# Biases of two small attention stages on VectorE, the shared expert summed in parts, routing weights carried with the expert rows

## The reference, cut to what matters

```python
# first attention: queries, and a second, small attention over the last 16 context rows
kv_dca = (y_dca @ Wkv_dca + bkv_dca).reshape(b, DCA, 2, H, HD)
k_dca = _ln(kv_dca[:, :, 0], kn_dca_w, kn_dca_b)
v_dca = kv_dca[:, :, 1]
q = _ln((x @ Wq + bq).reshape(b, s1, H, HD), qn_w, qn_b)
...
ctx = ctx + DCA_WEIGHT * _attn(qT, k_dca, v_dca)
# experts: top 2 of 16 for each token, at most 128 rows for each expert, and a shared expert
out = jnp.einsum('eci,edi->ecd', h, W2).astype(xt.dtype)
y_pairs = out[e, posc] * (w.reshape(-1) * valid)[:, None]
y = y_pairs.reshape(T, K, D).sum(axis=1)
shared = (silu(xt @ Ws1.T) * (xt @ Ws3.T)) @ Ws2.T
return y + shared
```

## Time and profile before

| | |
|---|---|
| time, median of 3 runs | 2241.15 us (2239.74 to 2242.74) |
| the profiled execution's own time | 2241.21 us |
| its span, first to last instruction | 2239.4 us |
| PE busy | 2004.3 us, 90% of the span |
| DVE busy | 1730.4 us, 77% |
| ACT busy | 1229.3 us, 55% |
| POOL busy | 1258.4 us, 56% |
| the three stages touched, first queries, small attention, experts | 37.6, 67.4 and 121 us long |

### The profile page before, as it was taken

How to read it: one execution, slowest core, us unless ns; L and a number is a source line. 1 busy time by engine, 2 the same in 40 slices (tenths; PEclk the granted TensorE clock), 3 DMA queues, 4 the chain that set the end, 5 groups by cost and what they waited for, 6 DMA issues and landing times. The chain is left out here.

```text
span 2239.4 us, 48991 instructions
## 1 busy us (share of the span) xinstructions
PE 2004.3 (90%) x17910; PEld 1649.8 (74%) x17910; DVE 1730.4 (77%) x2549; ACT 1229.3 (55%) x2124; POOL 1258.4 (56%) x1031
## 2 busy tenths in 40 slices
PE   6999999999999767999988785878999999999775
PEld 3788788878887555777777543657999999999763
DVE  5788888788888666888886434859899999999577
ACT  2788888888888513565655212664444444444443
POOL 0666666666666404545452041544898989898450
PEclk9999999999999866999999777989999999999988
DMA  2524222332332322434341343584222323231230
GB/s 87 175 99 167 113 113 112 153 128 98 130 135 115 129 73 90 176 126 168 133 153 58 116 135 90 158 209 143 102 102 103 109 94 116 81 118 38 90 128 17
DMA packets 117615, 262.18 MB, mean 117 GB/s; under 512 B 48033, under 2 KB 87106, under 8 KB 108338
## 3 DMA queue, kind: packets, MB, share of 16 engines
q1 hardware_dynamic: 113634, 248.88, 31.7%
q10 hardware_dynamic: 2304, 7.34, 0.8%
q0 software_dynamic: 1536, 3.94, 0.5%
HBM read 154.89 MB, written 109.20 MB: 118 GB/s over the span
## 5 line engine op out<-in xcount | busy, mean ns | idle before, releaser
L384 DVE TENSOR_REDUCE rk<-n_sq 128x1024 f32 (+2 forms) x384 | 465.8, 1213 | 124.1 <-ACT n_sq L332 121.6
L332 ACT ACTIVATE n_sq<-n_slot 128x1024 f32<-128x1024 f32 (+1 forms) x384 | 394.4, 1027 | 135.5 <-PE n_slot L292 126.3
L290 PE MATMUL n_slot<-n_wh,n_yh 128*128 128x512 f32 (+1 forms) x768 | 318.6, 415 | 2.0 <-PEq L485 2.0
L292 PE MATMUL n_slot<-n_wh,n_yl 128*128 128x512 f32 (+1 forms) x768 | 303.4, 395 | 0.0
L291 PE MATMUL n_slot<-n_wl,n_yh 128*128 128x512 f32 (+1 forms) x768 | 302.0, 393 | 0.0
L1441 POOL TENSOR_TENSOR p_S<-p_S,a_mb 128x896 f32<-128x896 f32 x94 | 255.3, 2754 | 68.0 <-ACT a_mb L1486 68.0
L1813 DVE TENSOR_REDUCE a_mpart<-a_pre 112x1 f32<-112x512 f32 (+1 forms) x384 | 238.7, 668 | 46.5 <-PE a_pre L1644 43.5
L1441 POOL TENSOR_TENSOR a_S<-a_S,a_mb 128x896 f32<-128x896 f32 (+1 forms) x89 | 240.7, 2741 | 39.5 <-ACT a_mb L1486 39.5
L1747 ACT ACTIVATE a_pr<-a_sc 128x896 f32<-128x896 f32 x192 | 171.8, 917 | 150.7 <-PE a_sc L1673 150.7
L264 POOL TENSOR_TENSOR n_khat<-n_kb,n_rs 128x240 f32<-128x240 f32 x192 | 114.7, 597 | 234.7 <-DVE n_rs L399 234.6
L1499 ACT ACTIVATE p_S<-p_S 128x896 f32<-128x896 f32 x96 | 91.5, 953 | 161.3 <-POOL p_S L1441 158.0
(11 more groups left out here) (395 smaller groups left out, 4729.9 us busy)
## 6 DMA issues: line engine op xcount, KB each, us to landing
vdram<-n_v SPq DMA_DIRECT2D x16, 1632.0 KB, 5.3
a_v<-vdram SPq DMA_DIRECT2D x16, 1632.0 KB, 6.7
kTdram<-n_kT SPq DMA_DIRECT2D x16, 1484.0 KB, 5.0
a_kT<-kTdram SPq DMA_DIRECT2D x16, 1484.0 KB, 7.5
n_yT<-in_ctxT SPq DMA_DIRECT2D x16, 750.0 KB, 9.1
yhdram<-n_yh SPq DMA_DIRECT2D x16, 750.0 KB, 6.4
yldram<-n_yl SPq DMA_DIRECT2D x16, 750.0 KB, 8.5
a_yh<-yhdram SPq DMA_DIRECT2D x16, 750.0 KB, 4.2
```

Of the source, the lines that this page charges most:

```text
L290: pe.matmul(dst, high, wh[:, cols], start=True, stop=False)
L292: mm = pe.matmul(dst, low, wh[:, cols], start=False, stop=True)
L332: act.activation(sq[0:n, w, :], slot[w][0:n, :], ACT.Square).then_inc(slot_free, 1)
L384: dve.tensor_reduce(g.rk[0:n, b, j, 8 * s:8 * s + 8], sq[0:n, (2 * j + s) % 3, :].rearrange("p (h d) -> p h d", h=8), X, ALU.add)\
```

## The change

It has five parts.

1. **First queries**: the bias matmul (512) goes; DVE adds the bias while it moves the bank into `z` (new function `bias`), ACT squares `z` instead of the bank, and the order of DVE's and ACT's steps is written anew. PE no longer waits for the table of ones; POOL does, in the next phase.
2. **Small attention, bias**: the bias matmul (670) goes; DVE adds a bias that is now stored on all 128 partitions.
3. **Small attention, loads**: `ydT`, `wkd`, `wvd` and the bias row are loaded by `load_splits` in the first layer norm, in front of the router's tables, and live until the small attention.
4. **Masked keys**: DVE makes half 0; half 1 is made by ACT in eight copies, one for each head, with the head's mask as a scale.
5. **Experts**: part 0 of the shared expert is multiplied for all 8 tiles before part 1, into four banks, and DVE adds two tiles at once; the routing weight travels as one more column of each row, is copied into `slot_w` beside the number, and is applied by ACT as it moves the expert's result; the last sums become four plain additions of four tiles each. POOL's scatter waits for the weights too, and SP's and ACT's waits for `pair_ready` count two copies for each expert.

```diff
-    for dst, src in ((g.blk, "blk"), (g.hmask, "hmask"), (g.bkdrow, "bkd")):
+    for dst, src in ((g.blk, "blk"), (g.hmask, "hmask")):
         sp.dma_start(dst[tuple(slice(None) for _ in dst.shape)], g.a[src]).then_inc(g.consts_in, 16)
+    for dst, src in ((g.ydT, "ydT"), (g.wkd, "L0_Wkd"), (g.wvd, "L0_Wvd"), (g.bkdrow, "bkd")):
+        sp.dma_start(dst[:, :], g.a[src]).then_inc(g.small_in, 16)
...
-                        pe.matmul(dst, g.xnT[:, k, t * TT:(t + 1) * TT], g.wqa[:, k, :], start=(k == 0), stop=False)
-                    mm = pe.matmul(dst, g.ones[0:1, 0:TT], g.qrow[0:1, 0, :], start=False, stop=True)
+                        mm = pe.matmul(dst, g.xnT[:, k, t * TT:(t + 1) * TT], g.wqa[:, k, :], start=(k == 0), stop=(k == 1))
...
+            def bias(s):
+                dve.wait_ge(q_psum, s + 1)
+                dve.tensor_tensor(of(z, s), ps[s][0:TT, :].rearrange("p (a n) -> p a n", a=GT),
+                                  g.qrow[0:TT, 0:1, :].broadcast_to([TT, GT, D]), ALU.add).then_inc(biased, 1)
...
-                pe.matmul(pt[:, t * D:(t + 1) * D], ydT[:, t * P:(t + 1) * P], wkd[:, :], start=True, stop=False)
-                mm = pe.matmul(pt[:, t * D:(t + 1) * D], g.ones[0:1, :], g.bkdrow[0:1, :], start=False, stop=True)
+                mm = pe.matmul(pt[:, t * D:(t + 1) * D], ydT[:, t * P:(t + 1) * P], wkd[:, :], start=True, stop=True)
...
+            act.wait_ge(kT_ready, 2)
+            for h in range(8):
+                act.activation(km[:, 1, :, h, :], kT[:, 1, :].rearrange("p (b k) -> p b k", b=B), ACT.Copy,
+                               scale=g.hmask[:, h:h + 1]).then_inc(km_ready, 1)
...
+            pool.wait_ge(w_ready, 1)
...
+            for t in range(NT):
+                pe.matmul(shared_out(t), hs[0][:, t * TT:(t + 1) * TT], w2a[:, E, :], start=(t % 2 == 0), stop=False,
+                          skip_group_check=True)
             pe.wait_ge(sh_steps, 8)
             for t in range(NT):
-                if t >= 2:
-                    pe.wait_ge(sh_added, t - 1)
...
+                mm = pe.matmul(shared_out(t), hs[1][0:FB, t * TT:(t + 1) * TT], w2b[:, E, :], start=False, stop=True,
+                               skip_group_check=True)
+                if t % 2 == 1:
+                    mm.then_inc(sh_out, 1)
+            pe.wait_ge(sh_added, NT // 2)
...
-                    act.activation(ye[1 - i][:, :], bY[1 - i][:, 0:D], ACT.Copy, scale=0.5).then_inc(y_ready, 1)
+                    act.activation(ye[1 - i][:, :], bY[1 - i][:, 0:D], ACT.Copy,
+                                   scale=slot_w[:, e:e + 1] if isinstance(e, int) else slot_w[:, bass.ds(e, 1)]).then_inc(y_ready, 1)
...
+                    dve.tensor_copy(slot_w[:, n:n + 1] if isinstance(n, int) else slot_w[:, bass.ds(n, 1)],
+                                    xe[i][:, D + 1:D + 2]).then_inc(pair_ready, 1)
...
-                    dve.scalar_tensor_tensor(out=g.x[:, t, :], in0=yg[:, k, t, :], scalar=w[:, k, t:t + 1],
-                                             in1=g.x[:, t, :], op0=ALU.mult, op1=ALU.add).then_inc(summed, 1)
+                    dve.tensor_tensor(g.x[:, tiles, :], g.x[:, tiles, :], yg[:, k, tiles, :], ALU.add).then_inc(summed, 1)
```

More of the change, by code:

```diff
@@ L243, in _ @@
             pool.wait_ge(set_up, 6)
+            pool.wait_ge(g.ones_in, 16)
             def step(b, i, pair):
@@ L556, in _ @@
             square(2)
+            root(2)
             high_part(0)
             square(3)
-            root(2)
             root(3)
@@ L605, in low_part @@
                                          op0=ALU.add, op1=ALU.subtract).then_inc(split, 1)
+            bias(0)
             sums(0)
+            bias(1)
             normalise(0)
             sums(1)
+            bias(2)
             normalise(1)
+            sums(2)
             low_part(0)
-            sums(2)
+            bias(3)
+            normalise(2)
             sums(3)
-            normalise(2)
             low_part(1)
@@ L632, in phase_dca @@
         S = lambda n: g.sem(f"d_{n}")
-        ydT, wkd, wvd = sb("ydT", [P, NKD]), sb("wkd", [P, D]), sb("wvd", [P, D])
+        ydT, wkd, wvd = g.ydT, g.wkd, g.wvd
         yrep = sb("yrep", [P, B, 8, DCA])
@@ L658, in _ @@
         def _(sp):
-            sp.dma_start(ydT[:, :], g.a["ydT"]).then_inc(y_in, 16)
-            sp.dma_start(wkd[:, :], g.a["L0_Wkd"]).then_inc(w_in, 16)
-            sp.dma_start(wvd[:, :], g.a["L0_Wvd"]).then_inc(w_in, 16)
             load_first_keys(sp, g)
@@ L787, in _ @@
                                   ALU.mult, ALU.mult).then_inc(kT_ready, 1)
-            dve.wait_ge(kT_ready, 2)
-            for half in range(2):
-                dve.tensor_tensor(km[:, half, :, :, :],
-                                  kT[:, half, :].rearrange("p (b k) -> p b k", b=B).unsqueeze(2).broadcast_to([P, B, 8, DCA]),
-                                  g.hmask[:, :].unsqueeze(1).unsqueeze(3).broadcast_to([P, B, 8, DCA]), ALU.mult)\
-                   .then_inc(km_ready, 1)
+            dve.wait_ge(kT_ready, 1)
+            dve.tensor_tensor(km[:, 0, :, :, :],
+                              kT[:, 0, :].rearrange("p (b k) -> p b k", b=B).unsqueeze(2).broadcast_to([P, B, 8, DCA]),
+                              g.hmask[:, :].unsqueeze(1).unsqueeze(3).broadcast_to([P, B, 8, DCA]), ALU.mult)\
+               .then_inc(km_ready, 1)
             p3 = lambda n: pr[n % 2][:, :, :, :].rearrange("p b h k -> p (b h) k")
@@ L2042, in phase_moe @@
         w2a, w2b = sb("w2a", [P, E + 1, D]), sb("w2b", [FB, E + 1, D])
-        xe = [sb(f"xe{i}", [P, D + 1]) for i in range(2)]
+        xe = [sb(f"xe{i}", [P, D + 2]) for i in range(2)]
         xeT, ye = [[sb(f"{n}{i}", [P, 2 * P]) for i in range(2)] for n in ("xeT", "ye")]
@@ L2340, in _ @@
             dve.wait_ge(side, 14)
-            dve.tensor_tensor(a3(w), a3(w), den[:, :].unsqueeze(1).broadcast_to([TT, 2, NT]), ALU.mult).then_inc(side, 1)
+            dve.scalar_tensor_tensor(out=rows[:, :, :, D + 1], in0=a3(w), scalar=0.5,
+                                     in1=den[:, :].unsqueeze(1).broadcast_to([TT, 2, NT]), op0=ALU.mult,
+                                     op1=ALU.mult).then_inc(w_ready, 1)
             for part in range(2):
@@ L2353, in _ @@
                     dve.tensor_tensor(h_, h_, ps[3 + half][0:m, 0:HALF], ALU.mult).then_inc(sh_steps, 1)
-            for t in range(NT):
-                dve.wait_ge(sh_out, t + 1)
-                dve.scalar_tensor_tensor(out=g.x[:, t, :], in0=ps[5 + t % 2][0:TT, 0:D], scalar=0.5, in1=g.x[:, t, :],
-                                         op0=ALU.mult, op1=ALU.add).then_inc(sh_added, 1)
+            for m in range(NT // 2):
+                dve.wait_ge(sh_out, m + 1)
+                xs = g.x[:, 2 * m:2 * m + 2, :]
+                dve.scalar_tensor_tensor(out=xs, in0=ps[SHARED[m]][0:TT, :].rearrange("p (a n) -> p a n", a=2), scalar=0.5,
+                                         in1=xs, op0=ALU.mult, op1=ALU.add).then_inc(sh_added, 1)
             def step(n, pair, i):
@@ L2384, in _ @@
                 pass
-            for t in range(NT):
+            for n in range(2):
+                tiles = slice(4 * n, 4 * n + 4)
+                dve.wait_ge(gathered[n], 32)
                 for k in range(2):
-                    dve.wait_ge(gathered[t // 4], 32)
-                    if t or k:
-                        dve.wait_ge(summed, 2 * t + k)
-                    dve.scalar_tensor_tensor(out=g.x[:, t, :], in0=yg[:, k, t, :], scalar=w[:, k, t:t + 1],
-                                             in1=g.x[:, t, :], op0=ALU.mult, op1=ALU.add).then_inc(summed, 1)
+                    if k:
+                        dve.wait_ge(summed, 2 * n + 1)
+                    dve.tensor_tensor(g.x[:, tiles, :], g.x[:, tiles, :], yg[:, k, tiles, :], ALU.add).then_inc(summed, 1)
 def ternary_weights(nc, g, ctx):
@@ L2680, in build @@
             with nc.sbuf_tensor("qs0", [P, T], F32) as qs0, nc.sbuf_tensor("qs1", [P, T], F32) as qs1, \
-                    nc.sbuf_tensor("cols", [P, 8], F32) as g.cols:
+                    nc.sbuf_tensor("cols", [P, 8], F32) as g.cols, nc.sbuf_tensor("ydT", [P, B * DCA], F32) as g.ydT, \
+                    nc.sbuf_tensor("wkd", [P, D], F32) as g.wkd, nc.sbuf_tensor("wvd", [P, D], F32) as g.wvd, \
+                    nc.sbuf_tensor("bkdrow", [P, D], F32) as g.bkdrow:
                 g.qs = [qs0, qs1]
@@ L2739, in laid_out @@
         "low": np.triu(np.ones((TT, TT), np.float32), 1),
[L2740 removed]
+        "L0_Wk": wk0, "L0_Wkd": wkd, "L0_Wvd": wvd, "ydT": i["ctx_1024"][:, SEQ - DCA:].transpose(2, 0, 1).reshape(C, B * DCA), "bk0": np.broadcast_to(bk0, (P, D)), "bkd": np.broadcast_to(bkd, (P, D)),
         "sel": sel, "den1": den1, "cols0": cols,
```

58 lines of the change are left out of this document (29 added, 29 removed).

## The result

The changed kernel takes 2217.99 us (median of 4 runs, 2216.02 to 2219.50), against 2240.44 for the kernel before, measured beside it: a ratio of 0.9899, 95% interval 0.9884 to 0.9914. The forecast was 2217.5. The profiled execution of the changed kernel took 2219.1 us, with a span of 2217.3, so the two traces differ by 22.1 us, and the table accounts for it. Every boundary in it is the first instruction of its kind in the trace.

The account below looks back on a forecast made before the run. Taken as last: PE in the first queries and small attention, PE's shared-expert matmuls in the experts, DVE in the last sums. Terms -5.6, -4.9, -1.3, -7.9, -4.1, +0.1 sum to -23.7 us; from 2241.21 that gave 2217.5, range 2211 to 2224.

Parts of the forecast that it names:

- First queries, gross: First queries without bias matmuls: DVE becomes last, the last reciprocal comes earlier; 7.0 us gained before the longer SP list.
- SP's list: Layer norm: three more load issues by SP put the first queries back by 1.4 us.
- Small attention: Its start: PE begins 3.3 us earlier, two bias matmuls save 2.3, a DVE step adds 0.72; net -4.9 us.
- The masked keys: Small attention: ACT's eight copies take 3.2 us beside DVE's half, so scores start 1.3 us earlier.
- Experts' start: First expert starts on its rows' landing, not behind the shared expert: -7.9 us, with +0.4 on the chain of rows.
- Last sums: End of the experts: sixteen DVE steps become four of 1024 columns, 1.2 us each; -4.1 us.
- The shared expert stayed last: Rival, experts' start: PE's clock falls or depth-48 matmuls run no faster, gain 3 instead of 7.9 us; 2222.4, chance 0.12.
- The far ends of the clock: Rival, touched stages: PE's clock rises later or earlier, 2213 to 2222; the far ends are the case, chance 0.12.
- SP's list did not eat the gain: Rival judged: early loads block SP, small attention's 3.3 us are paid back in the layer norm; 2219.5, chance 0.06.
- The copies of the weights cost nothing: Rival judged, experts: each expert's second copy costs more than DVE's 1.19 us idle per round; 2246 at 3 us, chance 0.02.

Follow-up runs that it names:

- e9: Kernel after, shared expert's depth-128 matmuls run twice: thrown away ahead of the gating, then behind it alternating with depth 48; 2218.51 us, 0.9914.
- e7: Kernel after, shared expert's second layer still grouped by depth but all behind the gating, so PE pauses ahead of it; 2219.48 us, 0.9902.
- e4: Kernel after, shared expert's second layer behind the whole gating, each tile's two matmuls side by side as before; 2230.59 us, 0.9953.

## Why the prediction was right, step by step

**What bounds the kernel.** Each stage had the engine last that was named, and the engine that took over was the right one in all four: DVE in the queries, PE without its DMA wait in the small attention, the rows' landing in the experts, the second half's landing in the sums.

**First queries, gross: 8.0 instead of 7.0.** The waits were foreseen (3.46 us in three places, 3.65 predicted). The mis-sized term is DVE's list. I counted every step of 512 columns at 0.72; where a step does not need the result of the one before it, it starts 0.60 behind (the sum at 26.93 and the bias at 27.53). From the first bias at 25.46 to the last reciprocal it is 17.0 us where 18.25 were counted. The PE side was much too cautious: 33.2 for the end of the tiles took 1.12 off each and kept the low pace, while in fact the clock rose. It did not matter, since DVE was last; with a faster DVE it would have been an error of 6 us (15.9 from the first matmul to the last tile, against 10.0).

**SP's list.** +1.4 was predicted; +1.0 in the profiled execution, 1.6 on average.

**Small attention.** PE's start, the two bias matmuls and the added DVE step: 5.2 us against 4.9. The masked keys: 1.20 measured by undoing them, 1.3 predicted, and the eight copies took 3.30 us for 3.2. One reading was wrong and cost nothing: the table load behind the copies was not "over long before the first scores", it ran from 784.07 to 785.35 beside them, ahead of the exponentials. By "ScalarE: Activation LUTs" of the Trainium skill, in its section on what a table load costs, eight copies were an estimated 3.3 us; the trace agrees. Its rule for kernel authors that multiplication belongs on VectorE holds for one copy (0.41 us against 0.28) and not for the stage, where the engine beside stood idle. Against DVE's half, 2.25 us, 3.3 is not "a third" more but nearly half.

**Experts' start.** -7.9 predicted, -8.28 + 0.35 = -7.93 found, and the landing is what releases PE. But the reason given was incomplete. "PE no longer pauses, so its clock need not fall" is one half, and grouping the depths is the other; either alone would have done it, as e9 and e7 show. The price of one matmul (0.50 us, half of 0.99; found 0.46) did not bind.

**Last sums: 3.15 instead of 4.1.** A step of 1024 columns is 1.24 us (1.2 predicted). The second half landed 3.2 us behind the first addition where I counted 2.8, which gives the stage 5.7 us instead of 5.2; and the first landed 5.99 us behind its issue, not 5.51, which the other traces show as spread.

**The rivals.** The shared expert stayed last in none of the runs with grouped matmuls. The far ends of the clock did not come, though the clock moved single stages by 1 us. "TensorE: Matmul & The Clock Gate" of the Trainium skill, in its section on oscillation, says that a wait for a DMA lets the clock fall ahead of the next burst. The traces agree, for a wait for DVE (e7 and e4 both start at the low level behind 3.2 us of it), but what it costs is between -0.25 and +8.4 us, by the order of the matmuls behind it. SP's list did not eat the gain. The copies of the weights cost nothing.

The total of the touched stages, -24.1, is 0.4 more than the -23.7 of the sum: one term was 1.0 too small, another 1.0 too large, and that they cancel is luck. The rest, to 22.1, is the +2.0 of stretches that nothing touched, which a sum of terms cannot foresee; that the median came within 0.5 us of 2217.5 all the same is luck too, since the profiled execution, at 2219.1, was 1.1 above it.

## What to carry to other kernels

Read a stage from its end, name who takes over when the last engine is relieved, and step through that engine's list with the pitch of its rows, not with their durations. Group matmuls by depth: here alternating depths cost a third more at the full clock, and behind a pause nearly two and a half times, since the low clock stayed. A wait that ends early is best judged by a stage's length in the trace: the time of the whole kernel moved by several us for reasons that no edit had.

## What the hardware showed that was not expected

- PE busy without a gap for 18 us (e4) stayed at a granted clock of 0.50, with depths of 128 and 48 side by side, and for 25 us (first queries of before) at the low pace, with depths of 128 and 1. Behind the same pause as in e4, the same products grouped by depth had the full clock back within 4 us (e7), still in the group of depth 128.
- At the full level a matmul of 112 x 256 took 0.46 us grouped, at either depth (0.43 within a group), and 0.61 alternating; at the low level 0.85 within a group and 1.12 alternating.
- The last store of the keys' stage took 6.49 us to land in one trace of twelve and 4.96 to 4.98 in the others, for the same 1484 KB; the whole stage waits for it.
- Where all the shared expert's work is over, POOL is now last in the experts' start. Its sixteen scatters come at a pitch of 1.24 us and end 1.6 us ahead of the first rows' load; nothing above touched them.

```profile
1276.24 0.94 POOL L2133 DMA_INDIRECT xbuf<-m_rows,m_su  x1 [0.30 <-issue]
1277.49 0.94 POOL L2133 DMA_INDIRECT xbuf<-m_rows,m_su  x1 [0.30 <-issue]
...
1293.67 0.94 POOL L2133 DMA_INDIRECT xbuf<-m_rows,m_su  x1 [0.31 <-issue]
```
